# Squared lengths of the distance groups in two fp32r halves, and the silu kept in its bank for the steps that VectorE weights

## The reference

```python
x = x + L0_attn(xn, ...) + L0_ffn(xn, ...)     # xn = layernorm(x)
x = x + L1_attn(xn, ...) + L1_ffn(xn, ...)
# L0_ffn: 64 experts of width 88 and a shared one of 176; top 8 of 64 per token
expert_out = vmap(lambda gw, uw, dw: silu(x @ gw.T) * (x @ uw.T) @ dw.T)(Wg, Wu, Wd)
routed = einsum('eth,te->th', expert_out, rw)          # rw: routing weights
# L1_attn, for each of 8 heads of 16 channels, window of 64 tokens:
dist = sqrt((diff * diff * m_h).sum(-1) + 1e-8)        # diff: key in the window less query
neg_d, loc = top_k(-dist, 32)
infl = exp(-topd); infl = infl / (infl.sum(-1) + 1e-8)
context = einsum('btk,btkd->btd', infl, neighbor_v)
```

## Time and profile before

| | |
|---|---|
| time, median of 3 runs | 739.52 us (737.44 to 740.01) |
| the profiled execution | 739.74 us |
| its span, first to last instruction | 737.9 us |
| mean granted TensorE clock | 0.962 |
| PE, DVE, ACT, POOL busy | 90%, 81%, 56%, 50% |

### The profile page before, as it was taken

How to read it: one execution, slowest core, us unless ns; L and a number is a source line. 1 busy time by engine, 2 the same in 40 slices (tenths; PEclk the granted TensorE clock), 3 DMA queues, 4 the chain that set the end, 5 groups by cost and what they waited for, 6 DMA issues and landing times.

```text
span 737.9 us, 12696 instructions
## 1 busy us (share of the span) xinstructions
PE 667.7 (90%) x3984; PEld 443.9 (60%) x3984; DVE 596.5 (81%) x2527; ACT 414.0 (56%) x759; POOL 367.5 (50%) x406
## 2 busy tenths in 40 slices
PE   3899999999999999999899999999999999889722
PEld 2555676666556666666556676666666566677621
DVE  3888657987986999899938999948759999549983
ACT  2555245467566847466557575454877463478600
POOL 2157255656553766456535955646634666222220
PEclk9999999999999999999998999999999999999955
DMA  9930000000000000000000000000100000010101
GB/s 288 365 95 1 0 1 0 1 0 1 23 12 1 10 11 18 8 13 17 17 1 1 11 13 16 14 6 2 25 9 10 16 13 16 4 42 26 34 19 28
DMA packets 25727, 21.99 MB, mean 30 GB/s; under 512 B 1920, under 2 KB 23596, under 8 KB 25148
## 3 DMA queue, kind: packets, MB, share of 16 engines
q1 hardware_dynamic: 25660, 21.18, 9.6%
HBM read 18.95 MB, written 2.23 MB: 29 GB/s over the span
## 4 chain that ended last, share of the span: by engine, by line
PE 48%; DVE 37%; issue 4%; POOL 4%; ACT 3%; DMA 2%; SPq 1%; DVEq 0%; ACTq 0%; POOLq 0%
PE bank_X L512 13%; PE bank_A L512 12%; PE bank_G L512 11%; PE bank_U L512 10%; DVE S L809 9%; DVE Wk L1233 9%; DVE m L1230 6%; DVE GWk L809 2%; DMA vw<-vscratch 2%; SPq L414 1%; DVE rr L809 1%; POOL S L1550 1%; DVE hg L817 1%; DVE Wlo L809 1%; PE bank_X L521 1%
## 5 line engine op out<-in xcount | busy, mean ns | idle before, releaser
L512 PE MATMUL bank_A<-S,WdT 128*128 128x512 f32 x368 | 188.0, 613 | 2.1 <-POOL S L1550 1.2
L1550 POOL TENSOR_TENSOR Wlo<-Wgu,Whi 128x256 fp32r<-128x256 f32 x138 | 110.1, 804 | 112.9 <-ACT Whi L1293 112.7
L1550 POOL TENSOR_TENSOR S<-S,Rb 128x512 f32<-128x512 f32 x88 | 117.4, 1335 | 94.7 <-DVE S L809 94.3
L809 DVE TENSOR_TENSOR S<-S,bank_U 128x512 f32<-128x512 f32 x184 | 124.0, 679 | 43.4 <-PE bank_U L512 27.2
L1293 ACT ACTIVATE S<-bank_G 128x512 f32<-128x512 f32 x184 | 107.7, 595 | 89.5 <-PE bank_G L512 80.0
L1293 ACT ACTIVATE Whi<-Wgu 128x256 fp32r<-128x256 f32 x184 | 74.9, 414 | 93.4 <-PE bank_U L512 83.2
L512 PE MATMUL bank_U<-xH,Whi 128*128 128x512 f32 x184 | 96.2, 523 | 9.1 <-DVE S L809 8.8
L512 PE MATMUL bank_G<-xH,Whi 128*128 128x512 f32 x184 | 98.3, 534 | 3.9 <-POOL Wlo L1550 2.1
L512 PEld LDWEIGHTS bank_A<-S,WdT 128*128 128x128 f32 x368 | 66.0, 192 | 40.0 <-issue 22.3
L1233 DVE MATCH_REPLACE8 Wk<-m,Wk 128x79 f32<-128x79 f32 x384 | 82.0, 225 | 0.0
L809 DVE TENSOR_TENSOR S<-S,Rb 128x512 f32<-128x512 f32 x88 | 76.6, 874 | 2.2
(11 more groups left out here) (238 smaller groups left out, 1177.8 us busy)
## 6 DMA issues: line engine op xcount, KB each, us to landing
vw<-vscratch SPq DMA_DIRECT2D x32, 158.0 KB
Wgu<-in_Wgu SPq DMA_DIRECT2D x2, 2048.0 KB, 15.1
xs<-in_x SPq DMA_DIRECT2D x4, 256.0 KB, 6.9
wqk<-in_w_qkv SPq DMA_DIRECT2D x1, 1024.0 KB, 7.4
Wgu<-in_Wgu SPq DMA_DIRECT2D x1, 1024.0 KB, 9.0
vscratch<-mo SPq DMA_DIRECT2D x4, 256.0 KB
out<-xs SPq DMA_DIRECT2D x3, 256.0 KB, 3.0
Wgu<-in_Wgu SPq DMA_DIRECT2D x1, 512.0 KB, 5.2
```

Source lines behind the costliest of these rows:

```text
L512: return engine.matmul(dst, lhsT, rhs, start=start, stop=stop)
L809: return engine.tensor_tensor(dst, a, b, op)
L1550: return engine.tensor_tensor(dst, a, b, op)
```

## The change

The side rows: the lengths of `nm` and `pq` are each kept as a high part, rounded to fp32r by a ScalarE copy, and the rest, which VectorE makes by a subtraction from the bank on the partitions that `negside` marks with -1. `Pk`, `La` and `Ra` are fp32r, with 64 + 16 + 16 rows of 128, and the opening matmul has fp32r operands. `La` is written in two pieces, and the first two groups wait for the first alone (`la`). The extras come by one load and are spread by three ScalarE copies (`sides`). In the last batch GpSimd makes all query operands.

The silu: for a weighted step with even n ScalarE writes the silu back to its bank. VectorE multiplies the bank by `Rb` into S, which frees G, and then multiplies S by U, which frees U; the down projection waits for U alone. The wait for a free ring buffer (`down`) moves from ScalarE to VectorE for these steps.

All five strings of `ORDER` are new; the diff shows SyncE's and the end of PE's.

```diff
--- before.py
+++ after.py
 SIDE = GT * NH
-AUX = SIDE + NH + TQ
+NEAR = 2 * SIDE
+MASK = NEAR + 2 * NH
...
     "sp":
-        "vvvvvvvvvvvvvvvvvvvvvvvvvvvvsvvsvsvvvvssvss",
+        "vvvvvvvvvvvvvvvvvvvvvvvvvvvvvvssvvvvsvvssss",
     "pe":
...
-        "eeeemeeteeetmmtmmeeeeetmeetmemeeeeeetmmmtmmthftftffthfhfhhfhfhhffffhhffdffddffdffdtdftdfdtfftffffttf"
-        "ttftfttttttttttt",
...
+        "meetemeeteetmeeemmmeteetemeeeemeemteemmmtmmthftftffthfhfhhffhhhfffhhfdffddddtfftdtftddfffttttftfttff"
+        "ttfftffttftttt",
...
+    put("negside", (p[:, None] // SIDE == 1) * -1.0 + ((p[:, None] >= NEAR + NH) & (p[:, None] < MASK)) * -1.0)
...
...
         hb = sb("hb", [64, 1])
-        nmx = sb("nmx", [128, NH + 128])
-        Pk = sb("Pk", [SIDE + NH, PADK + T])
-        La = sb("La", [AUX, NG, 128])
-        Ra = [sb(f"Ra{i}", [AUX, GT, WK]) for i in range(2)]
+        nmx = sb("nmx", [128, 2 * NH + GT * NEAR])
+        Pk = sb("Pk", [MASK, PADK + T], FR)
+        PQ = sb("PQ", [NEAR, 128], FR)
+        La = sb("La", [128, NG, 128], FR)
+        Ra = [sb(f"Ra{i}", [128, GT, WK], FR) for i in range(2)]
         hf = sb("hf", [128, T])
...
         heads4 = bd.rearrange("p (h t) -> p h t", h=NH).unsqueeze(1).to_broadcast([128, GT, NH, TQ])
-        pick4 = K("pick", SIDE).rearrange("p (h t) -> p h t", h=NH).unsqueeze(1).to_broadcast([SIDE, NG, NH, TQ])
+        pick4 = K("pick", NEAR).rearrange("p (h t) -> p h t", h=NH).unsqueeze(1).to_broadcast([NEAR, NG, NH, TQ])
...
         def queries_on_vector(b, g):
-            return g % 2 == 1
+            return g % 2 == 1 and b < B - 1
...
             load("ld_b", rr[1][:, :], d["w_proj"])
-            load("ld_e", La[SIDE:, :, :], d["extras"][SIDE:, 0:128].unsqueeze(1).to_broadcast([NH + TQ, NG, 128]))
-            for k in range(2):
-                load("ld_e", Ra[k][0:SIDE, :, :], d["extras"][0:SIDE, 128:].rearrange("p (a c) -> p a c", a=GT))
-                load("ld_e", Ra[k][SIDE + NH:, :, :],
-                     d["extras"][SIDE + NH:, 128:].rearrange("p (a c) -> p a c", a=GT))
+            load("ld_e", flat(Ed[0])[:, 0:128 + GT * WK], d["extras"])
...
                         pe.wait_ge("mo", m // NF)
-                    if weighted(m):
-                        pe.wait_ge("tw_v" if weight_on_vector(m) else "tw_p", weight_count(m))
+                    if weighted(m) and not weight_on_vector(m):
+                        pe.wait_ge("tw_p", weight_count(m))
                     else:
...
                 pe.wait_ge("nmx", b + 1)
-                mm(t[SIDE:SIDE + NH, :], nmx[:, 0:NH], ksq[:, :]).then_inc(sems(full(bank("nm", b))), 1)
+                mm(t[NEAR:MASK, :], nmx[:, 0:2 * NH], ksq[:, :]).then_inc(sems(full(bank("nm", b))), 1)
                 yield
                 t = fill("pq", b)
-                o = t[0:SIDE, 0:128].rearrange("p (g t) -> p g t", g=NG)
+                o = t[0:NEAR, 0:128].rearrange("p (g t) -> p g t", g=NG)
                 for i in range(GT):
                     q = ksq[:, :].rearrange("p (g a t) -> p g a t", g=NG, a=GT)[:, :, i, :]
-                    p = mm(o, nmx[:, NH + SIDE * i:NH + SIDE * i + SIDE], q, i == 0, i == GT - 1)
+                    p = mm(o, nmx[:, 2 * NH + NEAR * i:2 * NH + NEAR * i + NEAR], q, i == 0, i == GT - 1)
                 p.then_inc(sems(full(bank("pq", b))), 1)
...
                     pe.wait_ge("qb_v" if queries_on_vector(b, g) else "qb_p", query_count(b, g))
-                    pe.wait_ge(empty(bank("pq", b)), nth("pq", b) + 1)
+                    pe.wait_ge("la", 2 * b + (1 if g < 2 else 2))
                     pe.wait_ge("ra", b * NG + g + 1)
...
                         dve.wait_ge(empty(bank("sp", n // NF, k)), nth("sp", n // NF, k) + 1)
-                        dve.wait_ge(empty(bank("u", n)), nth("u", n) + 1)
-                        tt(s[:, :], s[:, :], Rb[k][:, :], ALU.mult).then_inc(sems("tw_v"), 1)
+                        dve.wait_ge("silu", weight_count(n))
+                        if n >= RING:
+                            dve.wait_ge("down", n - RING + 1)
+                        emptied(tt(s[:, :], Rb[k][:, :], ps("g", n)[:, :], ALU.mult), "g", n)
...
                 if b == B - 1:
+                    yield from lengths_of_keys(b)
                     yield from lengths_of_queries(b)
...
                 if b < B - 1:
+                    yield from lengths_of_keys(b)
                     yield from lengths_of_queries(b)
+            def lengths_of_keys(b):
+                yield
+                dve.wait_ge("pk_hi", b + 1)
+                t = filled("nm", b)
+                emptied(stt(Pk[NEAR:, PADK:], Pk[NEAR:, PADK:].bitcast(F), K("negside")[NEAR:MASK, :], t[NEAR:MASK, :],
+                            ALU.mult, ALU.add), "nm", b)
+
             def lengths_of_queries(b):
                 yield
+                dve.wait_ge("pq_hi", b + 1)
                 t = filled("pq", b)
-                dve.wait_ge("ld_e", 16 * 5)
+                a = emptied(stt(PQ[:, :], PQ[:, :].bitcast(F), K("negside", NEAR), t[0:NEAR, 0:128], ALU.mult, ALU.add),
+                            "pq", b)
+                dve.wait_ge(*a)
+                dve.wait_ge("sides", 3)
                 if b > 0:
                     dve.wait_ge(full(bank("dist", b - 1, NG - 1)), nth("dist", b - 1, NG - 1) + 1)
-                q = t[0:SIDE, 0:128].rearrange("p (g t) -> p g t", g=NG).unsqueeze(2).to_broadcast([SIDE, NG, NH, TQ])
-                a = tt(La[0:SIDE, :, :].rearrange("p g (h t) -> p g h t", h=NH), q, pick4, ALU.mult)
-                emptied(a, "pq", b)
+                for g in (slice(0, 2), slice(2, NG)):
+                    n = g.stop - g.start
+                    q = PQ[:, :].bitcast(F).rearrange("p (g t) -> p g t", g=NG)[:, g, :].unsqueeze(2)
+                    tt(La[0:NEAR, g, :].rearrange("p g (h t) -> p g h t", h=NH), q.to_broadcast([NEAR, n, NH, TQ]),
+                       pick4[:, g, :, :], ALU.mult).then_inc(sems("la"), 1)
+                    yield
...
                     t = filled("g", n)
-                    if n >= RING:
-                        sc_.wait_ge("down", n - RING + 1)
-                    emptied(act(S[n % RING][:, :], t[:, :], ACT.Silu), "g", n)
+                    if weighted(n) and weight_on_vector(n):
+                        act(t[:, :], t[:, :], ACT.Silu).then_inc(sems("silu"), 1)
+                    else:
+                        if n >= RING:
+                            sc_.wait_ge("down", n - RING + 1)
+                        emptied(act(S[n % RING][:, :], t[:, :], ACT.Silu), "g", n)
                     if n == total - 1:
...
                     for q in (m, m - 1):
-                        sc_.wait_ge("tw_v" if weight_on_vector(q) else "tw_p", weight_count(q))
+                        if weight_on_vector(q):
+                            sc_.wait_ge(empty(bank("g", q)), nth("g", q) + 1)
+                        else:
+                            sc_.wait_ge("tw_p", weight_count(q))
                 emptied(act(Rb[k][:, :], t[:, :], ACT.Copy), "sp", b, k)
...
                 emptied(act(HB[:, :], t[:, 0:128], ACT.Copy), "hb")
+                yield
+                sc_.wait_ge("ld_e", 16)
+                e = flat(Ed[0])[:, 0:128 + GT * WK]
+                act(La[:, :, :], e[:, 0:128].unsqueeze(1).to_broadcast([128, NG, 128]), ACT.Copy).then_inc(sems("sides"), 1)
+                yield
+                for k in range(2):
+                    act(flat(Ra[k]), e[:, 128:], ACT.Copy).then_inc(sems("sides"), 1)
...
                     sc_.wait_ge("ra", b * NG)
-                a = emptied(act(Pk[SIDE:, PADK:], t[SIDE:SIDE + NH, :], ACT.Copy), "nm", b)
-                sc_.wait_ge(*a)
-                act(Pk[SIDE:, 0:PADK], Pk[SIDE:, PADK:PADK + 1].to_broadcast([NH, PADK]), ACT.Copy).then_inc(
-                    sems("pk"), 1)
+                act(Pk[NEAR:, PADK:], t[NEAR:MASK, :], ACT.Copy).then_inc(sems("pk_hi"), 1)
+                yield
+                t = filled("pq", b)
+                if b > 0:
+                    sc_.wait_ge("la", 2 * b)
+                act(PQ[:, :], t[0:NEAR, 0:128], ACT.Copy).then_inc(sems("pq_hi"), 1)
+                yield
+                sc_.wait_ge(empty(bank("nm", b)), nth("nm", b) + 1)
+                act(Pk[NEAR:, 0:PADK], Pk[NEAR:, PADK:PADK + 1].bitcast(F).to_broadcast([2 * NH, PADK]),
+                    ACT.Copy).then_inc(sems("pk"), 1)
...
                     sc_.wait_ge("pk", b + 1)
-                    sc_.wait_ge("ld_e", 16 * 5)
+                    sc_.wait_ge("sides", 3)
                     if g >= 2:
                         sc_.wait_ge(full(bank("dist", b, g - 2)), nth("dist", b, g - 2) + 1)
-                    w = Pk[SIDE:, t0:t0 + WK]
-                    w = bass.AP(w.tensor, w.offset, [list(w.ap[0]), [TQ, GT], [1, WK]])
-                    act(Ra[k][SIDE:SIDE + NH, :, :], w, ACT.Copy).then_inc(sems("ra"), 1)
+                    w = Pk[NEAR:, t0:t0 + WK]
```

(21 more changed lines are left out.)

62 lines of the change are left out of this document (28 added, 34 removed).

## The result

| kernel | time, us: median (lowest to highest) | ratio to before, 95% interval |
|---|---|---|
| before | 738.48 (734.92 to 740.01) | 1 |
| after | 711.98 (709.46 to 712.73) | 0.9642 [0.9598, 0.9686] |

The change takes 26.5 us off, and the forecast was 13.7. The profiled execution of after took 709.46 us, its span 707.7.

A forecast was written before the change was run, and what follows sets the result against it. TensorE was taken to set the pace up to 634 us with VectorE close behind, then top-32 rounds and window transfers; 739.7 - 9.5 - 3.0 + 2.0 - 3.2 = 726.0 us, range 716 to 738.

The forecast's parts named there:

- opener in one pass: Matmul opening each distance group: one fp32r pass saves 0.53 us for 24 groups, three quarters credited, -9.5 us.
- product from the bank: 88 weighted products on VectorE read the bank, 679 instead of 874 ns; -3.0 us at the end.
- hold of G: Gate bank G stays held until VectorE's product, so TensorE's next gate matmul may wait: +2.0 us.
- tail: Last batch: window 2 issued sooner through query products on GpSimd, opener and order, less subtract and pad: -3.2 us.
- order, main part: Five rewritten engine lists: interleaving alone worth some 4 us either way, counted as range and not as a term.
- the bound on VectorE's saving: Of 13.4 us net saved on VectorE, between 0 and its 37/85 chain share, 5.9 us, reaches the end.
- rival C: Hold decides: gate banks found held cost TensorE 0.68 us each; slower, 763 us with 58 held; chance 0.10.
- the price of a store ahead of a window: SyncE's store ahead of window 7 takes 8.20 us to issue; taken to cost nothing while windows queue on one DMA engine.
- Rival D: Silu's return doesn't help: product mean stays 874 ns with a bank operand, +1.7 instead of -3.0, 730.7 us; chance 0.06.
- Rival A: Only TensorE's part at its low end, hold at its high end, VectorE's gain worth nothing: 732.2 us; chance 0.20.
- B: Rival: opener and VectorE gains both in full, 12.7 and 5.9 us, giving 717.9 us; chance 0.16.

The follow-up runs named there:

- SBUF pair with hold: Kernel after with silu written to S in SBUF and multiplied there, bank G still freed only by VectorE's weighting product: 726.06 us, ratio 0.9837.
- SBUF pair with and without: Kernel after with silu written to SBUF: G freed only by VectorE's weighting product, 726.06 us; G freed behind the silu, 723.03 us.
- both parts undone: Kernel after with silu to SBUF again and opener in two fp32 passes, new lists kept: 730.24 us, ratio 0.9885.

## Why the prediction was wrong

| term | forecast, us | measured, us | by which runs |
|---|---|---|---|
| opener in one pass | -9.5 (7.1 to 12.7) | -6.4; -6.1 in the old order | two passes against after; one pass against before |
| product from the bank | -3.0 (0 to -5.9) | -14.4 | SBUF pair with hold against after |
| hold of G | +2.0 (0 to 2.8) | +3.0, inside the noise | SBUF pair with and without |
| tail | -3.2 (0 to -5) | -8.0 | the two profiles |
| order, main part | 0 (±4) | -2.9 | both parts undone, its profile |

The measured terms sum to 28.7 us by these rows; by ratios the two parts and the rest are 18.0 + 8.5 = 26.5, the whole effect. The two sums differ by no more than the runs' spread.

**The step that failed is the bound on VectorE's saving**: "How much reaches the end is bounded by 0 [...] and by VectorE's share 37/85 of it, 5.9 us" (13.4 x 37/85 is 5.8). The saving itself was sized rightly, 0.195 us for each of 88 (in the new order 885 - 679 = 206 ns, 18.1 us). But some 14 us of it reached the end, as I had used the shares of the chain as a rate of exchange and as a bound. The runs show three things in its place. TensorE's idle time fell by more than the bound, by 9.2 us in the main part (SBUF pair with hold against after). VectorE's busy time fell by 24.4 us and not by 18.1. And GpSimd, for which no term stood, was busy 21.7 us less (377.1 to 355.4). Which of the two engines' gains carries the 14.4 us was not parted.

The way from the product to TensorE's wait is not shown either. With the pair in SBUF 22 of the 88 products last over 1000 ns, and they hold 16.3 of the 17.7 us above the median of 684. But of TensorE's ten waits for these products at G or U only two (0.8 and 0.3 us) come right behind a long one; what made VectorE late for the others was not followed. The waits for VectorE at U in the earlier trace rows, 5.9 us, were no measure of what the saving could bring.

**The opener**: 0.51 us were saved for each against 0.53 forecast, but this is the sum of one pass and filled rows. The pass alone saves 0.31 us in the new order (0.53 - 0.22), 7.4 us for 24 groups, of which 6.4 reached the end, and 0.39 in the old order, 9.4 us, of which 6.1 did. So the share of three quarters was about right and the term was 9.5 because the filled rows' part stood in it. That part belongs to the "order" row, since the version with both parts undone keeps the 128 rows; how much of its 2.9 us is that was not tried alone.

**The hold** was right in place in the new order, and its forecast size fits TensorE's 2.7 us of waits at G; the rival C that it fed was right of the old one. From the end of a silu to the start of its product pass 1.16 us in the mean in after and 2.02 us in the version with the old lists, where the product nearly always stands directly ahead of the one with U (0.72 us between their starts); in after a quarter of them start 1.9 us or more ahead of it. The forecast gave the order ±4 us. For this edit it is the sign: the same silu in its bank costs 24.5 us with the one set of lists and brings 11.5 with the other.

**The tail**: "the end is the issue of window 2 plus 59 us, and a later change of SyncE's order [...] moves nothing while the windows queue." The issue came only 1.3 us sooner where 3.2 were forecast (43.1 us behind the last down projection, before 44.4), and the constant, held to be fixed, fell: from 655.31 to 702.67, where window 7 lands (687.72 + 14.95 in the chain of after), six windows took 47.4 us instead of 54.2. Most of the tail's 8.0 us, 6.8, is this shorter time of the windows, for which the forecast had no term. In the trace of DMA packets, where only windows move, a packet of 512 bytes took about 27 ns in the kernels with after's lists and tiles and about 31 in those with before's; **why is open**, as lists and tiles were not parted. The 5.0 us of the query products and the 13.7 of SyncE's string are prices inside the new order and don't add up to the 8.0. The statement on SyncE's string is false in the new order (13.7 us) and true in the old one (0.0), where the store stood behind a window under way. The forecast named the price of a store ahead of a window, 8.2 us, and dropped it, as the windows kept their engine busy; that was right of the old order, and in the new one, where the store came 18 us behind window 2, it was not.

Rival D is refuted: no product of S with a bank operand lasts over 693 ns in any of the traces. The Trainium skill (SBUF — State Buffer, Who interferes with whom) has it that a two-input product contends with GpSimd only with both inputs in SBUF, and the traces agree, at 679 against 885 ns. Rival A, in which VectorE's gain is worth nothing, is refuted by the 14.4 us. B was nearest with 717.9, and not by its terms: it had 12.7 for the opener and 5.9 for the product, where 6.4 and 14.4 were measured.

## What to carry to other kernels

Where two engines are both over 80% busy, don't exchange busy time for end time by the shares of the chain, and don't take them for a bound: count too what the other engines gain from the same edit, and try it with the lists held fixed. Price a hold by how long the holding instruction stands in its engine's list, because the same edit gained 11.5 us with lists written for it and lost 24.5 without. Before costing a queue of transfers by its mean, ask how many DMA engines one transfer uses: one more row brought 7.2, 8.6 and 14.6 us in three kernels.

## What the runs showed of the hardware

- After 16 matmuls of one column (1.9 us) and an idle 3.5 us TensorE's granted clock was 0.50 for over 9 us (the silu in its bank, in the order of before). Behind the same 16 matmuls and no wait it was 0.76 and 0.82 in two cuts of 4 us (SBUF pair with hold).
- VectorE's product of two SBUF operands took 628 to 2228 ns beside GpSimd, one with a bank operand 628 to 690. GpSimd gained as well: its splits took 747 instead of 811 ns.
- ScalarE's silu takes 583 ns from a bank into the same bank and 593 into SBUF. The Trainium skill (ScalarE: Activation LUTs, Step-by-step: what each stage is for) calls PSUM the faster destination; the rows agree, by 10 ns.
- An fp32r matmul of 316 columns over 56 rows kept TensorE 0.34 us, over 128 rows 0.22, and the eight matmuls behind it took 1.12 and 1.01 us.
- A window of 79 rows took 9.0 us in before and 7.9 in after, one behind the other (54.2/6, 47.4/6); one of 80 rows landed 2.2 to 3.9 us after its issue.
